# A decoder layer on one core: stacked output projection, rotary halves swapped by VectorE, quantisation and last key chunk on GpSimd

## The reference, cut to what matters

```python
x = x + self_attention(layernorm(x))      # one head of 128, causal, rotary on q and k
#   rotary: oe = te*cos + to*sin ; oo = -te*sin + to*cos   (te, to: even and odd columns)
# cross attention, h = 16 heads
q = (layernorm(x) @ Wq) ; k = ctx @ Wk ; v = ctx @ Wv
attn = softmax(q k^T / 8) ; x = x + concat_h(attn @ v) @ Wo + bo
# feed forward with quantised input
x_int = clip(round(layernorm(x) / scale), -127, 127)
x = x + (x_int * scale) @ (ternary - 1).T + bias
```

## Time and profile before

| | us |
|---|---|
| three runs | 1163.97, 1164.08, 1164.45 |
| profiled execution, its own time | 1164.64 |
| its span (first to last instruction) | 1162.8 |
| TensorE matmuls busy | 1133.6 (97%) |
| VectorE busy | 936.3 (81%) |
| ScalarE busy | 695.2 (60%) |
| GpSimd busy | 231.6 (20%) |

### The profile page before, as it was taken

How to read it: one execution, slowest core, us unless ns; L and a number is a source line. 1 busy time by engine, 2 the same in 40 slices (tenths; PEclk the granted TensorE clock), 3 DMA queues, 4 the chain that set the end, 5 groups by cost and what they waited for, 6 DMA issues and landing times.

```text
span 1162.8 us, 17669 instructions
## 1 busy us (share of the span) xinstructions
PE 1133.6 (97%) x6561; PEld 1047.9 (90%) x6561; DVE 936.3 (81%) x1691; ACT 695.2 (60%) x1001; POOL 231.6 (20%) x228
## 2 busy tenths in 40 slices
PE   6799999999999999999999999999999999999996
PEld 5588999999999999999999999999999999999995
DVE  3698888887888888788978888887888888878645
ACT  1155656656565665756667565665656566575753
POOL 3120130221303022130302213030221302112010
PEclk9799999999999999999999999999999999999998
DMA  6101010010101001010010101001010100100000
GB/s 152 41 1 41 2 41 3 2 41 4 41 3 40 5 2 41 3 41 3 12 32 1 41 4 41 3 5 39 2 41 3 41 3 1 43 2 1 4 1 4
DMA packets 12707, 24.13 MB, mean 21 GB/s; under 512 B 4934, under 2 KB 8654, under 8 KB 12494
## 3 DMA queue, kind: packets, MB, share of 16 engines
q1 hardware_dynamic: 12622, 23.00, 7.4%
HBM read 21.88 MB, written 0.82 MB: 20 GB/s over the span
## 4 chain that ended last, share of the span: by engine, by line
PE 94%; DVE 3%; issue 1%; ACT 1%; DMA 0%; POOL 0%; POOLq 0%; DVEq 0%; ACTq 0%
PE banks L1062 36%; PE banks L1092 33%; PE banks L916 11%; PE banks L954 5%; PE banks L907 4%; PE banks L936 1%; PE banks L997 1%; PE banks L1025 1%; DVE maxes L642 1%; PE banks L987 1%; DVE pr_lo L863 0%; DVE maxes L650 0%; DVE xn L626 0%; PE banks L974 0%; PE banks L966 0%
## 5 line engine op out<-in xcount | busy, mean ns | idle before, releaser
L591 ACT ACTIVATE pr_hi<-banks 128x800 fp32r<-128x800 f32 x384 | 322.1, 839 | 384.7 <-PE banks L1062 384.7
L642 DVE TENSOR_REDUCE maxes<-banks 128x1 f32<-128x482 f32 x585 | 370.4, 652 | 62.7 <-PE banks L916 58.9
L863 DVE TENSOR_TENSOR pr_lo<-banks,pr_hi 128x800 fp32r<-128x800 f32 x320 | 314.8, 984 | 58.0 <-ACT banks L593 56.3
L593 ACT ACTIVATE banks<-banks 128x800 f32<-128x800 f32 x384 | 319.9, 833 | 0.0
L916 PE MATMUL banks<-cT_hi,q_hi 96*128 96x482 f32 x585 | 223.5, 382 | 1.4 <-DVE maxes L642 1.4
L1062 PE MATMUL banks<-q_hi,cT_hi 97*128 97x400 f32 x768 | 215.3, 361 | 2.9 <-DMA q_hi<-negmaxT 2.5
L1092 PE MATMUL banks<-pr_hi,cN_hi 128*97 128x400 f32 x768 | 214.1, 346 | 0.1
L1062 PE MATMUL banks<-q_hi,cT_lo 96*128 96x400 f32 x768 | 208.4, 352 | 0.0
L1062 PE MATMUL banks<-q_lo,cT_hi 96*128 96x400 f32 x768 | 204.1, 347 | 0.0
L1092 PE MATMUL banks<-pr_hi,cN_lo 128*96 128x400 f32 x704 | 190.8, 345 | 0.0
L1092 PE MATMUL banks<-pr_lo,cN_hi 128*97 128x400 f32 x704 | 190.5, 344 | 0.0
(11 more groups left out here) (116 smaller groups left out, 890.6 us busy)
## 6 DMA issues: line engine op xcount, KB each, us to landing
cT_raw<-in_ctxT SPq DMA_DIRECT2D x16, 568.5 KB
cN_raw<-in_ctx SPq DMA_DIRECT2D x16, 528.0 KB
out<-result SPq DMA_DIRECT2D x16, 50.0 KB
X<-in_x SPq DMA_DIRECT2D x1, 700.0 KB
cN_raw<-in_ctx_last SPq DMA_DIRECT2D x16, 40.5 KB
wqT<-in_wqT SPq DMA_DIRECT2D x1, 512.0 KB, 5.0
wo<-in_wo SPq DMA_DIRECT2D x1, 512.0 KB, 12.3
wkT<-in_wkT SPq DMA_DIRECT2D x1, 384.0 KB, 6.6
```

The source lines that it names most:

```text
L591: nc.scalar.activation(pr_hi[:, s % RING, :].rearrange("p (a q) -> p a q", a=2), pair, ACT.Exp, scale=float(DH) ** -0.5).then_inc(hi_done, 1)
L593: nc.scalar.activation(pair, pair, ACT.Exp, scale=float(DH) ** -0.5).then_inc(exp_done, 1)
L642: nc.vector.tensor_reduce(maxes[:, t, p:p + 1], here[:, 0:PW], AX.X, ALU.max).then_inc(misc_free, 1)
L863: nc.vector.tensor_tensor(pr_lo[:, s % RING, :].rearrange("p (a q) -> p a q", a=2), banks[:, slot:slot + 2, 0:BLK], pr_hi[:, s % RING, :]. ...
```

## The change

- Output projection: the 4 x 4 blocks of `o_sb` (4 blocks of 4 heads, 96 rows each) are stacked in `o_st`, 128 rows by 3 by 400 columns, by six DMAs; G is stacked the same way once, in `G_st`. y is then 12 matmuls with 128 rows instead of 16 with 96. The matmul of one (k, h) adds up rows that belong to different heads, which is what the sum over heads wants.
- The reciprocals go from 64 partitions to a row in DRAM and from there by six broadcasting DMAs into `r_st`, of the shape of `o_st`; GpSimd multiplies the two. `partition_broadcast` is gone. The reciprocals are taken in step 5 instead of 3.
- Rotary: only q and k are projected (two matmuls instead of four), and VectorE multiplies the swapped halves by the sine (two instructions of 64 partitions instead of one of 128).
- `normalize3` and the quantisation, and the last key chunk, go from VectorE to GpSimd. Their last use, behind the loop, stays on VectorE.

```diff
+STACKED = [(0, 0, 96, 0, 0), (1, 0, 32, 0, 96), (1, 32, 64, 1, 0), (2, 0, 64, 1, 64), (2, 64, 32, 2, 0),
+           (3, 0, 96, 2, 32)]
...
-        wself = sb("wself", [D, 5, D])
+        wself = sb("wself", [D, 3, D])
...
+            def move_sums(n, par, y_use):
 
                 sp.wait_ge(o_evac, NB * (n + 1))
-                sp.dma_start(sums[:, :], o_sb[par][DC:DC + 1, :].rearrange("p (h s) -> p h s", h=H)).then_inc(sums_in_s, 16)
+                sp.dma_start(sums[:, :], o_sb[par][DC:DC + 1, :].rearrange("p (h s) -> p h s", h=SP)).then_inc(sums_in_s, 16)
+                if y_use is not None:
+                    sp.wait_ge(misc_ready, y_use + 1)
+                for i, row, rows, k, to in STACKED:
+                    sp.dma_start(o_st[to:to + rows, k, :],
+                                 o_sb[par][row:row + rows, i * BLK:(i + 1) * BLK]).then_inc(ost_in_s, 16)
                 sp.wait_ge(recip_done, n + 1)
-                sp.dma_start(rrow[:, :].rearrange("p (h s) -> p h s", h=H), rsums[:, :]).then_inc(rrow_in_s, 16)
+                sp.dma_start(rrow.rearrange("(h s) -> h s", h=SP), rsums[:, :]).then_inc(rrow_in_s, 16)
+                sp.wait_ge(rrow_in_s, (n + 1) * 16)
+                for i, row, rows, k, to in STACKED:
+                    sp.dma_start(r_st[to:to + rows, k, :],
+                                 rrow[i * BLK:(i + 1) * BLK].rearrange("(a q) -> a q", a=1).to_broadcast([rows, BLK])).then_inc(rst_in_s, 16)
...
+            sp.wait_ge(g_done, 4)
+            for i, row, rows, k, to in STACKED:
+                sp.dma_start(G_st[to:to + rows, k, :, :], G[row:row + rows, 4 * i:4 * i + 4, :]).then_inc(gst_in_s, 16)
...
+                order.link(nc.gpsimd.tensor_scalar(last_part[:, :], last_hi[:, :].bitcast(F32), last[0:ROWS, 0:1], None, ALU.mult))
+                nc.gpsimd.tensor_tensor(out=cN_hi[par][0:ROWS, FULL, 0:DC], in0=last_part[:, :],
+                                        in1=cN_raw[0:ROWS, FULL, :], op=ALU.add).then_inc(last_done, 1)
...
-                order.link(nc.gpsimd.partition_broadcast(rball[:, :], rrow[:, :]))
-                nc.gpsimd.tensor_tensor(out=o_sb[par][0:DC, :], in0=o_sb[par][0:DC, :], in1=rball[:, :],
+                pool.wait_ge(ost_in_s, (n + 1) * 16 * len(STACKED))
+                pool.wait_ge(rst_in_s, (n + 1) * 16 * len(STACKED))
+                nc.gpsimd.tensor_tensor(out=o_st[:, :, :], in0=o_st[:, :, :], in1=r_st[:, :, :],
                                         op=ALU.mult).then_inc(on_done, 1)
...
+            def quantize(n):
+
+                pool.wait_ge(rstd_done[2], n + 1)
+                order.link(nc.gpsimd.tensor_scalar(xq[:, :], x2[:, :], mv3[:, 0:1], rs3[:, :], ALU.subtract, ALU.mult))
...
+                nc.gpsimd.tensor_scalar(xq[:, :], xq[:, :], MAGIC, scl[:, 2:3], ALU.subtract,
+                                        ALU.mult).then_inc(xd_done, 1)
...
+                    for to, of in ((slice(0, D // 2), slice(D // 2, D)), (slice(D // 2, D), slice(0, D // 2))):
+                        turned = nc.vector.tensor_tensor(rt2[to, :, :], v[of, :, :],
+                                                         sinT[of, :].unsqueeze(1).to_broadcast([D // 2, 2, S]), ALU.mult)
...
-                    if present(b, -1):
-                        if s == 15:
-                            normalize3(b - 1)
-                        if 16 <= s <= 18:
-                            quantize(s - 16)
...
-                    if s == 10 and present(b, 1):
-                        last_chunk(b + 1, 1 - par)
...
-                    if s == 3 and present(b, -1):
+                    if s == 5 and present(b, -1):
...
-                    for m in range(4):
+                    for m in range(2):
...
-                    for h in range(H):
-                        mm = nc.tensor.matmul(here[0:S, 0:D], o_sb[par][0:DC, h * S:(h + 1) * S], G[:, h, :],
-                                              start=(h == 0), stop=(h == H - 1))
+                    for h in range(4):
+                        for k in range(KB):
+                            mm = nc.tensor.matmul(here[0:S, 0:D], o_st[:, k, h * S:(h + 1) * S], G_st[:, k, h, :],
+                                                  start=(h == 0 and k == 0), stop=(h == 3 and k == KB - 1))
```

More of the change, by code:

```diff
@@ L65, in decoder_layer @@
     QB = H // 4
+    KB = 4 * DC // P
     PARTS = 4
@@ L69, in decoder_layer @@
     QMAX = 127.0
+    SP = 64
     FLT_MAX = 3.4028234663852886e38
@@ L114, in decoder_layer @@
         last = sb("last", [P, 2])
+        last_part = sb("last_part", [ROWS, DC])
         cT_raw = sb("cT_raw", [DC, NT])
@@ L124, in decoder_layer @@
         negmaxT = sb("negmaxT", [QT, P], F32R)
-        sums = sb("sums", [H, S])
-        rsums = sb("rsums", [H, S])
+        sums = sb("sums", [SP, Q // SP])
+        rsums = sb("rsums", [SP, Q // SP])
         o_sb = two("o_sb", [DC + 1, Q])
-        rrow = sb("rrow", [1, Q])
-        rball = sb("rball", [DC, Q])
+        rrow = nc.dram_tensor("rrow", [Q], F32).ap()
+        G_st = sb("G_st", [P, KB, 4, D])
+        o_st = sb("o_st", [P, KB, BLK])
+        r_st = sb("r_st", [P, KB, BLK])
         st1, st2, st3 = (sb(f"st{i}", [S, 6]) for i in (1, 2, 3))
@@ L176, in decoder_layer @@
         const_s = sem("const_s")
+        gst_in_s, ost_in_s, rst_in_s = sem("gst_in_s"), sem("ost_in_s"), sem("rst_in_s")
         mg_ready = sem("mg_ready")
@@ L201, in decoder_layer @@
         wffn_done = sem("wffn_done")
+        scl_done = sem("scl_done")
         pchain = sem("pchain")
@@ L401, in body @@
                 if present(b, -1):
-                    move_sums(b - 1, 1 - par)
+                    move_sums(b - 1, 1 - par, use_of(b - 1, "y") if present(b, -2) else None)
                 if present(b, 2):
@@ L495, in ffn_input @@
                 nc.gpsimd.tensor_tensor(out=x2b[:, :], in0=x2[:, :], in1=fb_bc[:, :], op=ALU.add).then_inc(x2b_done, 1)
+            def quantize(n):
+                pool.wait_ge(rstd_done[2], n + 1)
+                order.link(nc.gpsimd.tensor_scalar(xq[:, :], x2[:, :], mv3[:, 0:1], rs3[:, :], ALU.subtract, ALU.mult))
+                order.link(nc.gpsimd.tensor_scalar(xneg[:, :], xq[:, :], scl[:, 3:4], 0.0, ALU.mult, ALU.min))
+                order.link(nc.gpsimd.tensor_scalar(xq[:, :], xq[:, :], scl[:, 3:4], 0.0, ALU.mult, ALU.max))
+                order.link(nc.gpsimd.tensor_scalar(xq[:, :], xq[:, :], QMAX, None, ALU.min))
+                order.link(nc.gpsimd.tensor_tensor(out=xq[:, :], in0=xq[:, :], in1=xneg[:, :], op=ALU.add))
+                order.link(nc.gpsimd.tensor_scalar(xq[:, :], xq[:, :], -QMAX, MAGIC, ALU.max, ALU.add))
+                nc.gpsimd.tensor_scalar(xq[:, :], xq[:, :], MAGIC, scl[:, 2:3], ALU.subtract,
+                                        ALU.mult).then_inc(xd_done, 1)
             for n in (0, 1):
@@ L523, in body @@
                     ffn_input(b - 1)
+                    if b == 1:
+                        pool.wait_ge(scl_done, 1)
+                    quantize(b - 1)
             batches(body)
@@ L666, in consume @@
                 elif what == "QK":
-                    v = here[:, 0:4 * S].rearrange("p (a m s) -> p a m s", a=2, m=2)
+                    v = here[:, 0:2 * S].rearrange("p (a s) -> p a s", a=2)
                     at_least(dve, rope_done, n)
[L670 to L674, removed]
+                    order.mark(nc.vector.tensor_tensor(rt[:, :, :], v, cosT[:, :].unsqueeze(1).to_broadcast([D, 2, S]),
+                                                       ALU.mult))
+                    for to, of in ((slice(0, D // 2), slice(D // 2, D)), (slice(D // 2, D), slice(0, D // 2))):
+                        turned = nc.vector.tensor_tensor(rt2[to, :, :], v[of, :, :],
+                                                         sinT[of, :].unsqueeze(1).to_broadcast([D // 2, 2, S]), ALU.mult)
+                    turned.then_inc(misc_free, 1)
                     dve.wait_ge(misc_free, use + 1)
@@ L749, in high_T @@
                 nc.vector.tensor_copy(cT_hi[par][0:DC, keys], cT_raw[:, keys]).then_inc(cThi_done, 1)
[L751 to L756, removed]
             def normalize3(n):
@@ L819, in _ @@
             link(nc.vector.reciprocal(scl[:, 3:4], scl[:, 3:4]))
-            link(nc.vector.tensor_scalar(scl[:, 2:3], scl[:, 0:1], 1e-5, FLT_MAX, ALU.max, ALU.min))
+            nc.vector.tensor_scalar(scl[:, 2:3], scl[:, 0:1], 1e-5, FLT_MAX, ALU.max, ALU.min).then_inc(scl_done, 1)
             dve.wait_ge(x_rest_s, 16)
@@ L938, in fill @@
                 elif what == "V":
-                    mm = nc.tensor.matmul(here[0:S, 0:D], xnT[par][:, :], wself[:, 4, :], start=True, stop=True)
+                    mm = nc.tensor.matmul(here[0:S, 0:D], xnT[par][:, :], wself[:, 2, :], start=True, stop=True)
                 elif what == "S":
@@ L952, in fill @@
                     pe.wait_ge(on_done, n + 1)
-                    for h in range(H):
```

(13 more changed lines are left out.)

5 lines of the change are left out of this document (removed).

## The result

| kernel | median us | runs | ratio to before, 95% interval |
|---|---|---|---|
| before | 1164.00 | 6 (1163.80 to 1164.45) | 1 |
| changed | 1144.62 | 6 (1144.49 to 1144.69) | 0.9833 [0.982, 0.9846] |
| forecast | 1143.5 | range 1140.3 to 1149.0 | |

A forecast was written before the change was run, and what follows sets the result against it. TensorE, full in the batches, was taken as the bound. Terms of 13.1, 6.1 and 1.7 us (20.9) off the profiled 1164.64 gave 1143.7, 1143.2 with the median 0.56 lower; forecast 1143.5 us, range 1140.3 to 1149.0.

The forecast's parts named there:

- y: Output projection, 16 matmuls to 12: 0.875 us shorter in each of 15 batches, -13.1 us (-14.7 to -11.1).
- QK: Rotary's projections in the batches, 4 matmuls to 2: 0.435 us less in each of 14 batches, -6.1 us.
- the sum: Savings of y, QK and The start together, 20.9 us, with nothing lost elsewhere; chance 0.76.
- The start: Two QKs at the kernel's start: 2.02 us saved, 0.28 us more on VectorE between them, -1.7 us (0 to -2.0).
- The middle: Stretch from first y to last y, with 14 y and 12 QK: 17.5 us gained.
- What y waits for: Reciprocals, six broadcasts and multiplication before y: room 5 to 8 us, in the last batch 2 to 5, cost nothing.
- GpSimd's share: Quantisation's seven instructions on GpSimd, 3.2 us up to double, and the last chunk: ready in time, cost nothing.
- The exclusive wait: GpSimd and VectorE lock a shared port pair: at most 4 us a batch, inside VectorE's 10.75 us of room.
- A: Rival: new TensorE waits for low parts or maxima give back a quarter of the batches' saving, 4.8 us: 1148.3; chance 0.13.
- D: Rival: clock recovers sooner at the start and y's matmuls take 105 ns, 24.0 us gained: 1140.1; chance 0.05.
- B: Rival: the six broadcasts before y are late, y waits 4.8 us 15 times: 1215; slower if over 14 us; chance 0.04.
- C: Rival: quantisation is late on GpSimd, a wait of 2 us in 15 batches: 1173 us; chance 0.02.

The follow-up runs named there:

- rows_96: The changed kernel with its 12 matmuls of y over 96 of the 128 stacked rows, the other 32 left out: 1144.47 us.
- qk_alone: The kernel before with only the rotary change, two projections instead of four and halves swapped by VectorE: 1157.33 us.
- y_alone: The kernel before with only the stacked output projection and what feeds it; rotary, quantisation and last chunk as before: 1151.55 us.
- rst_twice: The changed kernel with the six broadcasts of the reciprocals issued, waited for and issued again, GpSimd waiting for all twelve: 1145.55 us.
- rst_serial: The changed kernel with each of the six broadcasts of the reciprocals waited for before the next is issued: 1162.96 us.
- vector_quant: The changed kernel with quantisation and last chunk back on VectorE: 1144.72 us.
- quant_late: The changed kernel with the second instruction of the quantisation done 12 times instead of once on GpSimd: 1191.12 us.

## Why the prediction was right, point by point

- **The bound.** TensorE is full before and after, and all of the gain is matmuls that aren't there. Shown by the windows, and by the two parts alone, which add up to the whole (19.7 us, the whole 19.4).
- **y.** Forecast 0.875 us a time and 13.1 in all; the chain shows 0.88 (3.50 to 2.62), the part alone 12.75. That rows cost nothing was argued from V and AO, and is shown by rows_96.
- **QK.** Forecast 0.435 us a time, on the chain 0.45 (0.87 to 0.42). With the start's share the part alone gave 7.0 (7.4 between the profiled executions), the sum had 7.8; what is missing there is the start's.
- **The start.** Here the term was too large: 1.7 forecast, 1.27 came. I halved two pieces of the chain that hold a fixed part (2.02 us for 8 instructions, 1.16 for 4: 0.86 saved each time, not 1.01), and put 0.28 us for a step of VectorE that became 0.51 us longer. The input also came 0.12 us later in this execution. That makes 1.09 us; 0.18 more came between there and the first scores, and no run says why. The pace of half that the prediction read off these rows is right, though the clock column reads 1.00 there (8 to 12 us): eight instructions of one kind take 1.95 us at 11.84 (L1013) and 1.96 at 49.98 (L1023), where the column reads 0.50. Before its first change it was no guide to the pace.
- **The middle.** 17.11 instead of 17.5 us. The chains place the 0.4 us. Over the 12 batches from the first y to the thirteenth, 168.34 to 989.52 before and 166.34 to 972.14 after, a batch went from 68.43 to 67.15 us, 1.28 less where 1.31 was forecast; the last two became 0.87 and 0.86 shorter, as forecast for y alone.

```profile
989.52 3.50 PE banks L954 x32
```

```profile
972.14 2.62 PE banks L980 x24
```

In the same way a batch of qk_alone takes 67.99 us, 0.44 less, all that was forecast, and one of y_alone 67.63, 0.81 less instead of 0.875. So the loss goes with the stacked projection or what feeds it, not with the rotary. It is not on a wait of TensorE that the trace shows; its cause stays open.

- **What y waits for.** The six broadcasts fell into their bounds, the multiplication took 2.79 us for 2.73, and the room was 8.1 and 4.8 us where 5 to 8 and 2 to 5 were forecast. That the room is real is shown by rst_twice (+0.9), that it ends by rst_serial (+18.3, with 14.4 us for the broadcasts instead of 6.1).
- **GpSimd's share.** Forecast nothing; vector_quant gave nothing. The seven instructions took 0.46 to 0.80 us, inside the 0.45 to 0.9 that was allowed.
- **The exclusive wait.** It was weighed as harmless in the loop, and is (vector_quant is no slower or faster); at the start it cost the changed kernel 1.8 us. The kernel before has the same pair at the same place (2.20 us beside 2.25), so it dropped out of the difference; nothing was moved there.
- **The rivals.** A would have given back a quarter of the saving; 0.4 us of it went. D's earlier clock and 105 ns did not come (109 ns, and the mean clock of 0.99 is that of before). B and C did not occur, but both were priced one for one, a microsecond of wait for a microsecond of time, and that is too low. C has 1173 us for waits of 2 us in 15 batches; quant_late had just these, and took 1191, mostly since the clock fell behind seven of them. In rst_serial 12.4 us of waits cost 18.1. B's point of decision, "over 14 us", is where rst_serial came out (14.4 us, level with the kernel before), but that is partly luck: y waited 0.6 us in the middle and not the 1.3 that B's upper bound gives, and 2.8 us of the price was the clock.
- **The size.** The forecast's median is 1.1 us too low: 0.9 is the sum, as above. The 0.56 us between the profiled execution and the median, taken off as well, did not recur (1144.63 and 1144.62), and rounding up by 0.3 gave back half of that.

## What to carry to other kernels

Where TensorE is full, count its instructions and read each one's price from the chain; a contraction of 96 rows costs what one of 128 does, and restacking it by DMA cost next to nothing here as long as the data came before their place in the order. When a product is halved where the next step waits for its end, halve only what repeats, not the fixed part. A wait of TensorE can have a second price beyond its length, the pace after it. And a long instruction may be a wait in disguise: look at what another engine does beside it before moving anything else.

## What the runs showed of the hardware

- A float32 matmul of 128 columns is two instructions of 109 ns each, with 96, 100 or 128 rows.
- A VectorE `tensor_scalar` of 0.34 us took 2.16 us beside a GpSimd `tensor_tensor` of 2.25 us that had begun 0.17 us earlier.
- TensorE idle for 2.0 to 2.2 us once in some 70 us (30.4 us in 15 waits) led to a granted clock of 1.2 GHz for some 3.5 us in 7 of 15 batches of one execution, and not in the others. Idle for some 0.6 us a batch in the 14 batches of rst_serial it kept 2.4 GHz; idle for 4.2 us in the last one it fell.
- Six transfers, 614 KB together, from one row in DRAM to 128 partitions, took 6.1 us issued together and 14.4 us one by one.
- GpSimd's `tensor_scalar` of 100x128 took 0.54 us with one operation of a constant, and 0.72 to 0.80 us with two operations and a scalar per partition; its `tensor_tensor` 0.46 us.
